# Second cross-attention of a fused two-layer kernel: key tiles taken in pairs, self-attention steps placed anew

## The chip, the cores and the metric

One Trainium2 chip, one core. The metric is the device time of one launch in microseconds; lower is better. The kernel before takes 3031.07 us (median of 3 runs, 3030.28 to 3032.9).

## The reference, cut to what matters

x is 32 sequences of 64 rows of 256; ctx is 32 contexts of 1601 keys of 256. Each of six layer parts has a layer norm ahead and a residual around it. Layer 0 is a cross-attention over ctx, a causal self-attention and a quantised FFN; layer 1 is the part at issue, and a mixture-of-experts FFN follows it.

```
# layer 1, cross-attention: 16 heads of 16
kv = mem @ W_kv;  q = x @ W_q
attn = softmax(q k^T * 16**-0.5)          # 64 queries x 1601 keys per head
out  = (attn @ v) @ W_proj + b_proj       # x += out
# layer 1, self-attention: 16 heads of 16, causal, 64 rows
Q, K, V = per-head products of xn with Wq, Wk, Wv
attn = softmax(mask(Q K^T * 16**-0.5));  out = attn @ V
x += (out, transposed and reshaped) @ W_O
```

## The kernel before, in words

Five engine programs (PE, ACT, DVE, POOL, SP) are written out by hand, each in its own order; they meet only at semaphores, and an engine that waits holds all that stands behind it. x is held in SBUF as 16 tiles of 128 rows, two batches each. Phase B, the subject here, runs `pe_pair`, `act_pair`, `vec_pair` and `pool_pair` once per tile: 16 pairs of batches. The first pair has no tile to finish, the last has none to prepare.

A batch has two stages. In the **maxima stage** PE multiplies the queries by all keys in 16 units (`maxima`, L1133) for DVE to take row maxima, and between the units projects keys and values of the next batch (`project`, pieces K and V, into banks 6 and 5); ACT evacuates them (`evac`), POOL makes the low parts `k_lo` (`split_keys`, L527). It ends with DVE writing `shift`. In the **score stage** (PE L1278 to L1295) 13 key tiles `t` of 128 keys follow. "Scores" of a tile are 2 bf16 matmuls that lay down the shift (L1283) and 12 fp32r matmuls (L1287), all on 64 rows of the array, in two row groups side by side; they fill banks 0, 1 or 2, 3 (`t % 2`). ACT takes the exponential of the tile, 128x1024, into `probs` (L825). "Weigh" of a tile is 16 fp32 matmuls of 64 columns on 32 columns of the array (L1153, each recorded as two), four column groups side by side, into bank 4. PE's order is scores(t), weigh(t-1), then `finish(g)` and `prepare(g)` with `g = 13 * batch + t`.

`finish` spreads over both batches what is left for the tile before: at g=0 the output projection of the cross-attention (L1173); DVE adds it and the bias to x and takes the layer norm; g=2 the transposition of xn (L957), g=3 Q, K, V (L1183, L1185), and then four quarters q of four heads: S4(q), the scores of the self-attention (L1195, one fp32 matmul 128x128 by 512 columns, at g=4, 6, 8, 10), which needs `skbd`, the keys spread by head by POOL (`spread_keys`, L553). On DVE masking (L1672), maximum (L1675), and its negative (L1677); on ACT four exponentials with sums accumulated (L790); on PE the transposition P4T(q) (L1203, g=6, 8, 10, 12); on ACT its copy (L794); on PE the product with V, O4(q) (L1214, g=7, 9, 11, 13); on DVE a copy (L1686); on PE the transposition O4T(q) (L1218, L1222), on DVE the division into `cat` (L1691), and at g=16 the product with W_O (L1232).

`prepare` makes the queries of the next tile: layer norm at g=17, 18, transposition at g=19, PE's product at g=20 (L1244), that is at t=7 of the second batch. ACT copies it (L802, L804), POOL makes `q_lo` (`split_queries`) and then `qbd_hi` and `qbd_lo` (`spread_queries`, L540), on which the next pair's first maxima wait (L1252, L1253). In between ACT rounds the next context to `ctx_hi` in four parts (`round_ctx`, L767, after tiles 1, 2, 6, 7) and POOL makes `ctx_lo` (`split_ctx`, L533); SP loads `ctx_raw` again when two parts are done. POOL's order at the end of a pair is split_ctx(2), split_ctx(3), split_queries, spread_queries(0).

Of the kernel before, what the change touches and what calls it, by code (L numbers as in the profile page):

```python
# [71 lines left out]
CTX_STEPS = (1, 2, 6, 7)  # L72
PROBS = 3
# [42 lines left out]
def build(nc, io, out):  # L116
    ctx = ExitStack()
    with ctx:
# [28 lines left out]
        attn_ch = sb("attn_ch", [P, KT, P])  # L147
# [3 lines left out]
        bias_p = sb("bias_p", [P, D])  # L151
# [62 lines left out]
        inv_sb = sb_b("inv", [P, D])  # L214
        attn4 = sb_b("attn4", [P, 4, P])
# [5 lines left out]
        hq_buf = sb("hq_buf", [P, 2048])  # L221
        identb = sb("identb", [P, P], BF16)
# [53 lines left out]
        skbd = [sideB[:, 1792 + 512 * n:2304 + 512 * n].rearrange("p (h t) -> p h t", h=HPQ) for n in range(2)]  # L276
        v4 = sideB[:, 2816:3088]
        p4T = sideB[:, 3072:3584].rearrange("p (h t) -> p h t", h=HPQ)
        k_raw = [sideB[:, 768 + 512 * n:1280 + 512 * n] for n in range(2)]
        wkv_raw = probs[:, 0, :]  # L280

        def vals_of(n, t):
            all_of = vals[:, n, 0:KEY_TILES * HEADS * VW].rearrange("p (t h d) -> p t h d", h=HEADS, d=VW)
            return all_of[:, t, :, :]

# [7 lines left out]
        def unit_parts(m):  # L293
# [9 lines left out]
            qkv_ps qkv_ready ss_ps snmax_ready sp_ready spT_ps spT_ready so_ps  # L303
# [4 lines left out]
            po_ps sqkv_ps sqkv_ready skbd_ready s4_ps s4_masked p4_ready p4T_ps p4T_ready o4_ps weighed4_ready o4T_ps cat_ready wo_ps  # L308
# [19 lines left out]
            (wo[:, :, :], io["w_o"]), (bias_p[:, :], io["b_p"]), (convw[:, :, :], io["conv_w"]), (convb[:, :], io["conv_b"])]  # L328
# [9 lines left out]
        def _(sp):  # L338
# [20 lines left out]
            for h in range(HEADS):  # L359
                g, j = divmod(h, 4)  # L360
                sp.dma_start(w_cp4[32 * j:32 * j + HD, g, :], io["w_cp"][h % HPT * HD:h % HPT * HD + HD, h // HPT, :]).then_inc(s.cp_in, 16)

# [55 lines left out]
        def _(g):  # L418
# [29 lines left out]
            g.wait_ge(s.consts_ready, NCONST)  # L448
            g.memset(w_cp4[:, :, :], 0.0).then_inc(s.cp_zero, 1)
# [73 lines left out]
            bt = (qb, sqk, s4p, scp, ctp, kp)  # L523
# [29 lines left out]
            def spread_keys(q):  # L553

                a, h = divmod(q * HPQ, HPT)
                if q >= 2:
                    g.wait_ge(s.s4_ps, s4p.up())
                g.tensor_tensor(skbd[q % 2], skT[:, a, None, :].broadcast_to([P, HPQ, P]),  # L558
                                head_of[:, h:h + HPQ, None].broadcast_to([P, HPQ, P]), ALU.mult).then_inc(s.skbd_ready, 1)

            def pool_pair(first, last):
# [19 lines left out]
                if not last:  # L581
# [3 lines left out]
                    rsqrt()  # L585
                    split_ctx(2)
# [65 lines left out]
        def _(act):  # L652
# [124 lines left out]
            def finish(g):  # L777

                if g == 2:
                    copy_xnT(7)  # L780
                if g == 3:
# [4 lines left out]
                if g in (5, 7, 9, 11):  # L786
                    n = (g - 5) // 2 % 2
                    act.wait_ge(s.s4_masked, T["s4"].up())
                    for k in range(HPQ):
                        act.activation(s4[n][:, k, :], s4[n][:, k, :], ACT.Exp, bias=s4_nmax[n][:, k:k + 1], scale=HD ** -0.5,  # L790
                                       accum_out=s4_sum[n][:, k:k + 1]).then_inc(s.p4_ready, 1)
                if g in (6, 8, 10, 12):
                    act.wait_ge(s.p4T_ps, T["p4T"].up())
                    act.copy(p4T.rearrange("p h t -> p (h t)"), bank(7)).then_inc(s.p4T_ready, 1)  # L794

            def prepare(g):

                if g == 19:
                    copy_xnT(7)
                if g == 20:  # L800
                    act.wait_ge(s.qB_ps, T["qB"].up())
                    act.mul(qT.rearrange("p k t -> p (k t)"), bank(7, 256), HD ** -0.5).then_inc(s.qB_ready, 1)  # L802
                    act.wait_ge(s.qB_ready, T["qmul"].up())
                    act.copy(q_hi[:, :, :].rearrange("p k t -> p (k t)"), qT.rearrange("p k t -> p (k t)")).then_inc(s.q_hi_ready, 1)  # L804
# [5 lines left out]
            def act_pair(first, last):  # L810
                for b in range(2):
# [9 lines left out]
                    for t in range(KEY_TILES):  # L821
                        g = b * KEY_TILES + t
                        rows = slice(0, keys_of(t))
                        act.wait_ge(s.sc_ps, T["sc"].up())
                        act.activation(probs[rows, t % PROBS, :], PS[rows, 1024 * (t % 2):1024 * (t % 2) + 1024],  # L825
                                       ACT.Exp).then_inc(s.pr_ready, 1)
                        if not first:
                            finish(g)
                        if not last:
                            if g == 20:  # L830
                                act.wait_ge(s.qbd_lo_ready, T["qbd"].up())
                                T["qbd"].up()
# [8 lines left out]
            prepare(19)  # L841
            prepare(20)
# [15 lines left out]
            for g in range(17):  # L858
                finish(g)
# [62 lines left out]
        def _(pe):  # L922
# [5 lines left out]
                         attn=dict(B=2), sums=dict(B=2), sqkv=dict(B=3), skbd=dict(B=QUARTERS), s4_masked=dict(B=QUARTERS), p4=dict(B=QUARTERS * HPQ), p4T=dict(B=QUARTERS),  # L928
# [230 lines left out]
            def end_batch(n, fin):  # L1159

                pe.wait_ge(s.sums_ready, T["sums"].up())
                if n == 0 and fin:
                    pe.wait_ge(s.p4T_ready, T["p4T"].now() + 1)
                pe.matmul(bank(7, D), spread[:, :, :].rearrange("p j d -> p (j d)"), sums_sb[:, :], start=True, stop=True).then_inc(s.den_ps, 1)

            def finish(g):

                if g == 0:

                    pe.wait_ge(s.attn_ready, T["attn"].up(2))  # L1170
                    pe.wait_ge(s.cp_in, 16 * HEADS)
# [3 lines left out]
                if g == 2:  # L1175
                    transpose_xn(7)
                if g == 3:
# [9 lines left out]
                if g in (4, 6, 8, 10):  # L1187
                    q = (g - 4) // 2
                    if q == 0:
                        pe.wait_ge(s.k_lo_ready, T["k_sb"].now())  # L1190
# [14 lines left out]
                if g in (7, 9, 11, 13):  # L1205
                    q = (g - 7) // 2
                    if q:
                        pe.wait_ge(s.weighed4_ready, T["weighed4"].up())
                    if q in (0, 3):
                        pe.wait_ge(s.v_ready, T["v_sb"].now())  # L1210
                    pe.wait_ge(s.p4T_ready, T["p4T"].up())
                    for k in range(HPQ):
                        mine = (q * HPQ + k) * HD
# [3 lines left out]
                    if q:  # L1217
# [747 lines left out]
```

## Time and profile before

| | |
|---|---|
| median of 3 runs | 3031.07 us |
| the profiled execution's own time | 3030.97 us |
| its span, first to last instruction | 3029.2 us |
| PE, PEld busy | 2598.6 us (86%), 2161.2 us (71%) |
| DVE, ACT, POOL busy | 1550.3 (51%), 1403.8 (46%), 930.9 us (31%) |

Busy times of PE are modelled from records of pipelined matmuls, so in this document PE's order is read by starts: from the start of one group to the start of the next. A row "x32" merges 32 instructions. "[0.61 <-POOL ...]" is idle time ahead of the row and what ended it.

### The profile page before, as it was taken

What the parts mean: (1) busy time and instruction counts of PE and PEld (TensorE: products, weight loads), DVE (VectorE), ACT (ScalarE), POOL (GpSimd) and SP (SyncE); (2) the same over time, 40 slices, a digit from 0 to 9 for tenths busy, and PEclk for the clock granted to TensorE, in tenths of its full rate; (3) what the DMA queues carried; (4) which work ended last, traced back from release to release, by engine and by line L of the source; (5) the groups of instructions that cost most, each with busy time, mean ns of one, the idle gap of its engine ahead of it and who ended that gap; (6) DMA issues with size and microseconds to landing.
All of it is one profiled execution on the core that took longest, in us unless ns stands there. A gap on an engine that the chain in (4) does not pass through costs nothing.

```text
span 3029.2 us, 75593 instructions
## 1 busy us (share of the span) xinstructions
PE 2598.6 (86%) x32048; PEld 2161.2 (71%) x32052; DVE 1550.3 (51%) x2693; ACT 1403.8 (46%) x2563; POOL 930.9 (31%) x867
## 2 busy tenths in 40 slices
PE   6999832248999999999999999999999973699997
PEld 3555411137888888888888888888888743699997
DVE  3443377724445355455454454454454534477775
ACT  1222211125555555655655656656556431456564
POOL 1000034243443442442443443443433202211121
PEclk9999955569999999999999999999999965799999
DMA  8888500031110110100100101101101002466665
GB/s 346 316 317 314 224 0 0 0 112 42 35 35 23 35 34 23 37 32 23 45 24 25 44 23 34 35 23 35 34 23 35 2 1 96 155 215 203 213 198 154
DMA packets 48581, 270.19 MB, mean 89 GB/s; under 512 B 4896, under 2 KB 23584, under 8 KB 33696
## 3 DMA queue, kind: packets, MB, share of 16 engines
q1 hardware_dynamic: 40160, 255.82, 23.4%
q0 software_dynamic: 8160, 10.29, 2.2%
q8 instruction: 237, 3.88, 0.5%
q14 instruction: 24, 0.20, 0.0%
HBM read 247.58 MB, written 20.61 MB: 89 GB/s over the span
## 4 chain that ended last, share of the span: by engine, by line
issue 38%; PE 27%; POOL 21%; DVE 6%; DMA 3%; ACT 3%; POOLq 1%; SPq 0%; DVEq 0%; ACTq 0%
POOL k_lo L530 7%; POOL ctx_lo L538 6%; PE PS L1025 3%; PE PS L1005 3%; PE PS L1365 2%; PE PS L1366 2%; PE PS L1367 2%; POOL sideB L558 2%; POOL qbd_lo L543 2%; DMA unit_raw<-in_experts 1%; PE PS L1287 1%; PE PS L1382 1%; POOL slots_d L633 1%; PE PS L1384 1%; PE PS L1383 1%
## 5 line engine op out<-in xcount | busy, mean ns | idle before, releaser
L1634 DVE TENSOR_REDUCE mpart<-PS 128x1 f32<-128x802 f32 (+1 forms) x512 | 487.8, 988 | 443.2 <-PE PS L1141 443.0
L825 ACT ACTIVATE probs<-PS 128x1024 f32<-128x1024 f32 (+1 forms) x416 | 425.1, 1022 | 241.9 <-PE PS L1287 236.9
L530 POOL TENSOR_TENSOR k_lo<-sideB,k_hi 128x400 fp32r<-128x400 f32 (+1 forms) x256 | 255.2, 997 | 353.7 <-ACT k_hi L761 353.3
L538 POOL TENSOR_TENSOR ctx_lo<-ctx_raw,ctx_hi 128x801 fp32r<-128x801 f32 x128 | 224.6, 1764 | 430.2 <-ACT ctx_hi L773 430.2
L1287 PE MATMUL PS<-qbd_hi,k_hi 64*128 64x256 f32 (+1 forms) x1664 | 312.1, 372 | 0.0
L1141 PE MATMUL PS<-k_hi,qbd_hi 128*128 128x512 f32 (+2 forms) x1024 | 263.0, 359 | 22.8 <-POOL ctx_lo L538 13.7
L1153 PE MATMUL PS<-probs,vals 128*32 128x64 f32 x13312 | 272.9, 222 | 3.0 <-ACT probs L825 2.2
L760 ACT COPY sideB<-PS 128x400 f32<-128x400 f32 (+1 forms) x256 | 126.6, 494 | 275.4 <-PE PS L1121 275.4
L1153 PEld LDWEIGHTS PS<-probs,vals 128*32 128x32 f32 x13312 | 205.3, 109 | 66.5 <-ACT probs L825 14.0
L1128 PE MATMUL PS<-wkv_hi,ctx_hi 128*128 128x256 f32 (+1 forms) x832 | 236.4, 284 | 0.0
L1130 PE MATMUL PS<-wkv_hi,ctx_lo 128*128 128x256 f32 (+1 forms) x832 | 234.3, 282 | 0.0
L1287 PE MATMUL PS<-qbd_hi,k_lo 64*128 64x256 f32 (+1 forms) x1664 | 233.9, 278 | 0.0
L1287 PE MATMUL PS<-qbd_lo,k_hi 64*128 64x256 f32 (+1 forms) x1664 | 233.6, 277 | 0.0
L1129 PE MATMUL PS<-wkv_lo,ctx_hi 128*128 128x256 f32 (+1 forms) x832 | 233.2, 280 | 0.0
L763 ACT COPY vals<-PS 128x512 f32<-128x512 f32 x192 | 113.0, 589 | 214.2 <-PE PS L1130 214.2
L1141 PEld LDWEIGHTS PS<-k_hi,qbd_hi 128*128 128x128 f32 x1024 | 177.6, 192 | 47.4 <-DVE mpart L1634 24.7
L1365 PE MATMUL PS<-xT_hi,unit_hi 128*128 128x256 f32 x736 | 209.1, 284 | 2.2 <-DVE xT_lo L1848 2.2
L1366 PE MATMUL PS<-xT_lo,unit_hi 128*128 128x256 f32 x736 | 209.3, 284 | 0.0
L1367 PE MATMUL PS<-xT_hi,unit_lo 128*128 128x256 f32 x736 | 208.8, 284 | 0.0
L1119 PE MATMUL PS<-ctx_hi,wkv_hi 128*128 128x400 f32 (+1 forms) x512 | 186.9, 365 | 18.6 <-POOL ctx_lo L538 18.6
L644 POOL DMA_INDIRECT sum_d<-scaled,xg x46 | 75.8, 1647 | 347.7 <-DVE scaled L1885 340.7
L1121 PE MATMUL PS<-ctx_hi,wkv_lo 128*128 128x400 f32 (+1 forms) x512 | 178.4, 348 | 0.0
(324 smaller groups left out, 6174.3 us busy)
## 6 DMA issues: line engine op xcount, KB each, us to landing
unit_raw<-in_experts SPq DMA_DIRECT2D x46, 1536.0 KB, 7.1
ctxN<-in_ctxN SPq DMA_DIRECT2D x16, 3328.0 KB, 10.8
ctxT<-in_ctxT SPq DMA_DIRECT2D x16, 3204.0 KB, 10.4
ctx_raw<-in_ctxT SPq DMA_DIRECT2D x64, 801.0 KB, 4.5
slots_d<-pad_rows SPq DMA_DIRECT2D x2, 2990.0 KB, 18.5
xg<-slots_d SPq DMA_DIRECT2D x23, 260.0 KB, 2.8
x<-in_x SPq DMA_DIRECT2D x1, 2048.0 KB, 9.6
sum_d<-x SPq DMA_DIRECT2D x1, 2048.0 KB, 6.3
```

What stands on the lines that cost most here:

```text
L530: g.tensor_tensor(k_lo[:, n, a, c:c + width], k_raw[p % 2][:, 0:width], k_hi[:, n, a, c:c + width].bitcast(F32), ALU.subtract).then_inc(s. ...
L538: g.tensor_tensor(ctx_lo[:, a, cols], ctx_raw[:, cols], ctx_hi[:, a, cols].bitcast(F32), ALU.subtract).then_inc(s.ctx_lo_ready, 1)
L825: act.activation(probs[rows, t % PROBS, :], PS[rows, 1024 * (t % 2):1024 * (t % 2) + 1024], ACT.Exp).then_inc(s.pr_ready, 1)
L1128: pe.matmul(to, ctx_hi[:, k, keys], wkv_hi[:, k, D:2 * D], start=k == 0, stop=False)
L1130: mm = pe.matmul(to, ctx_lo[:, k, keys], wkv_hi[:, k, D:2 * D], start=False, stop=k == KT - 1)
L1141: mm = pe.matmul(at, qbd_hi[:, n, pair // 4, (pair % 4) * P:(pair % 4) * P + P], k_hi[:, n, pair // 4, c:c + width], start=True, stop=True)
L1153: mm = pe.matmul(bank(4, S, slice(32 * j, 32 * j + 32), g * S), vals[rows, n, mine:mine + 32], probs[rows, t % PROBS, at_head(h):at_head(h ...
L1287: mm = pe.matmul(bank(2 * (t % 2) + r, 256, rows, a * 256), keys_part[part, n, a, keys], queries[part, n, a, r * 256:r * 256 + 256], start ...
L1365: pe.matmul(to, hi[:, k, cols], tokens_hi[:, k, :], start=k == 0, stop=False)
L1366: pe.matmul(to, hi[:, k, cols], tokens_lo[:, k, :], start=False, stop=False)
L1367: mm = pe.matmul(to, lo[:, k, cols], tokens_hi[:, k, :], start=False, stop=k == KT - 1)
L1634: v.tensor_reduce(mpart[:, pair, half:half + 1], PS[:, at:at + width], AX, ALU.max).then_inc(s.mx_red, 1)
```

## The change

On PE the score stage takes the key tiles two by two: scores(t), scores(t+1), `beside(t)`, weigh(t-2), weigh(t-1), `beside(t+1)`, where `beside` calls `finish` and `prepare` with a place of 14 to a batch. `probs` gets a fourth buffer. S4 becomes two matmuls of 64 rows by 256 columns, side by side in banks 5 and 6, and `skbd` is half as wide. P4T(3) and what follows move into the second batch, and the queries' product from after 8 tiles' scores and 7 tiles' weighing to after 10 and 6. On ACT both exponentials of a pair stand ahead of the steps; the exponentials of a quarter are one instruction, for which DVE now subtracts the maximum and sums (`centre`, `sums4`). `round_ctx` runs after tile pairs 0 (two parts), 6 and 8. The projection's bias comes in as a row of its weights, which takes one DVE addition away. `k_raw` lies in `probs[1]`. POOL waits for the layer norm before it goes on.

```diff
-CTX_STEPS = (1, 2, 6, 7)
-PROBS = 3
+CTX_AT = {0: (0, 1), 6: (2,), 8: (3,)}
+PROBS = 4
+PLACES = KEY_TILES + 1
+S4_AT = (6, 8, 10, 12)
+P4T_AT = (8, 10, 12, PLACES + 2)
+O4_AT = (9, 11, 13, PLACES + 3)
+O4T_AT = (11, 13, PLACES + 3, PLACES + 5)
+WO_AT = PLACES + 6
+QUERY_AT = (PLACES + 7, PLACES + 8)
...
             def pool_pair(first, last):
...
                     rsqrt()
+                    g.wait_ge(s.xn_ready, xnp.up())
...
+            def exp_p4(q):      # ACT
+                act.wait_ge(s.s4_centred, T["s4"].up())
+                act.activation(s4[q % 2], s4[q % 2], ACT.Exp, scale=HD ** -0.5).then_inc(s.p4_ready, 1)
...
+                if window in (8, 10, 12, PLACES + 2):
+                    copy_p4T()
+                if window in (6, 8, 10, PLACES):
+                    exp_p4((6, 8, 10, PLACES).index(window))
...
+                    for t in range(0, KEY_TILES, 2):      # ACT
+                        for one in range(t, min(t + 2, KEY_TILES)):
+                            rows = slice(0, keys_of(one))
+                            if one == 1:
+                                act.wait_ge(s.k_lo_ready, T["k_lo"].now())
+                            act.wait_ge(s.sc_ps, T["sc"].up())
+                            act.activation(probs[rows, one % PROBS, :], PS[...], ACT.Exp).then_inc(s.pr_ready, 1)
                         if not first:
-                            finish(g)
+                            finish(b * PLACES + t)
                         if not last:
-                            prepare(g)
-                            if t in CTX_STEPS:
-                                round_ctx(CTX_STEPS.index(t))
+                            prepare(b * PLACES + t)
+                            for part in CTX_AT.get(t, ()):
+                                round_ctx(part)
...
+                if place in S4_AT:      # PE
+                    q = S4_AT.index(place)
...
+                    elif q == 1:
+                        pe.wait_ge(s.s4_masked, T["s4_masked"].up())
                     else:
-                        pe.wait_ge(s.s4_masked, T["s4_masked"].up())
+                        pe.wait_ge(s.weighed4_ready, T["weighed4"].up())
                     pe.wait_ge(s.skbd_ready, T["skbd"].up())
-                    pe.matmul(bank(6), sqT[:, q // 2, :], skbd[q % 2].rearrange("p h t -> p (h t)"), start=True, stop=True)
+                    for r in range(2):
+                        part = slice(64 * r, 64 * r + 64)
+                        mm = pe.matmul(bank(5 + r, 2 * P), sqT[part, q // 2, :], skbd[q % 2][part, :, :]..., skip_group_check=True)
...
                 pe.wait_ge(s.shift_ready, T["shift"].up(4))
-                for t in range(KEY_TILES):
+                def scores(t):
...
+                    if t >= 2:
+                        pe.wait_ge(s.pr_ready, exps_before + t - 1)
...
-                    if t >= 1:
-                        weigh(n, t - 1)
-                    if not first:
-                        finish(n * KEY_TILES + t)
-                    if not last:
-                        prepare(n * KEY_TILES + t)
+                for t in range(0, KEY_TILES, 2):
+                    for one in range(t, min(t + 2, KEY_TILES)):
+                        scores(one)
+                    beside(n * PLACES + t)
+                    if t:
+                        weigh(n, t - 2)
+                        weigh(n, t - 1)
+                    beside(n * PLACES + t + 1)
...
+            def centre(q):      # DVE
+                v.wait_ge(s.s4_masked, T["masked"].up())
+                v.tensor_reduce(s4_max, s4[q % 2], AX, ALU.max).then_inc(s.vec_step, 1)
+                v.wait_ge(s.vec_step, own())
+                v.tensor_tensor(s4[q % 2], s4[q % 2], s4_max[:, :, None].broadcast_to([P, HPQ, P]), ALU.subtract).then_inc(s.s4_centred, 1)
+            def sums4(q):
+                v.wait_ge(s.p4_ready, T["p4"].up())
...
+                v.tensor_reduce(s4_sum[q % 2], s4[q % 2], AX, ALU.add).then_inc(s.vec_step, 1)
+                v.wait_ge(s.vec_step, own())
+                v.reciprocal(s4_inv[q % 2], s4_sum[q % 2]).then_inc(s.vec_step, 1)
...
+                if window == 8:
+                    mask_keys(1)
+                    centre(1)
+                    sums4(0)
+                    take(0)
+                if window == 10:
+                    mask_keys(2)
+                    centre(2)
+                    sums4(1)
+                    take(1)
+                    divide(0)
+                if window == 12:
+                    mask_keys(3)
+                    sums4(2)
+                    take(2)
+                    divide(1)
+                if window == PLACES:
+                    centre(3)
```

## Rows read from the trace of the kernel before

**Rows 1.** Busy time by stretch, a pair's two score stages: window, length, engines, clock, DMA.
```profile
1261.18:1293.35 32.17, 31.46 (x638) 23.85 (x639) 10.04 (x27) 24.33 (x57) 11.93 (x10) 1.00 0.17 54
...
1320.51:1345.68 25.17, 25.12 (x605) 20.56 (x605) 2.82 (x10) 16.79 (x21) 12.40 (x10) 1.00 0.21 68
```
**Rows 2.** PE in order of time, first batch: start, us, engine, line, operation, count.
```profile
1264.14 0.39 PE L1283 MATMUL PS<-shift,onesb 64*128 64x512 bf16 x2
...
1273.27 1.10 PE L1195 MATMUL PS<-sideB 128*128 128x512 f32 x2 [0.61 <-POOL sideB L558]
...
1275.90 0.39 PE L1283 MATMUL PS<-shift,onesb 64*128 64x512 bf16 x2
...
1276.60 0.28 PE L1287 MATMUL PS<-qbd_lo,k_hi 64*128 64x256 f32 x2
1276.71 0.28 PE L1287 MATMUL PS<-qbd_hi,k_lo 64*128 64x256 f32 x2
1276.92 0.65 PE L1153 MATMUL PS<-probs,vals 128*32 128x64 f32 x32
1277.51 1.12 PE L1195 MATMUL PS<-sideB 128*128 128x512 f32 x2
1278.47 0.60 PE L1203 MATMUL PS<-ident,sideB 128*128 128x128 f32 x4
1279.00 0.39 PE L1283 MATMUL PS<-shift,onesb 64*128 64x512 bf16 x2
...
1290.15 0.65 PE L1153 MATMUL PS<-probs,vals 128*32 128x64 f32 x32
...
1290.62 0.40 PE L1214 MATMUL PS<-sideB 128*32 128x128 f32 x8
...
1291.21 0.41 PE L1283 MATMUL PS<-shift,onesb 64*65 64x512 bf16 x2
```
**Rows 3.** PE in order of time, end of the second batch.
```profile
1336.35 1.16 PE L1244 MATMUL PS<-xnT,w_cq 128*128 128x128 f32 x8
...
1344.97 0.65 PE L1153 MATMUL PS<-probs,vals 128*32 128x64 f32 x32
1345.68 0.61 PE L1141 MATMUL PS<-k_hi,qbd_hi 128*128 128x512 f32 x2
```
**Rows 4.** ACT in order of time, both batches.
```profile
1265.28 1.02 ACT L825 ACTIVATE probs<-PS 128x1024 f32<-128x1024 f32 x1 [1.93 <-PE PS L1287]
...
1279.11 0.59 ACT L794 COPY sideB<-PS 128x512 f32<-128x512 f32 x1 [0.22 <-PE PS L1203]
1279.59 0.86 ACT L773 CAST ctx_hi<-ctx_raw 128x801 fp32r<-128x801 f32 x1
1280.35 1.03 ACT L825 ACTIVATE probs<-PS 128x1024 f32<-128x1024 f32 x1
1281.27 0.40 ACT L790 ACTIVATE sideB<-sideB,small 128x128 f32<-128x128 f32 x1
...
1337.55 0.38 ACT L802 ACTIVATE sideB<-PS 128x256 f32<-128x256 f32 x1 [0.64 <-PE PS L1244]
```
**Rows 5.** DVE in order of time, first batch.
```profile
1274.40 0.69 DVE L1672 TENSOR_TENSOR sideB<-PS,causal 128x512 f32<-128x512 f32 x1 [7.00 <-PE PS L1195]
1275.13 0.69 DVE L1675 TENSOR_REDUCE small<-sideB 128x4 f32<-128x512 f32 x1
1275.85 0.17 DVE L1677 TENSOR_SCALAR small<-small 128x4 f32<-128x4 f32 x1
...
1280.96 0.29 DVE L1686 COPY xnT<-PS 128x128 f32<-128x128 f32 x1 [0.56 <-PE PS L1214]
```
**Rows 6.** POOL in order of time, end of the second batch, and the next first batch.
```profile
1339.21 1.61 POOL L538 TENSOR_TENSOR ctx_lo<-ctx_raw,ctx_hi 128x801 fp32r<-128x801 f32 x1 [1.55 <-ACT ctx_hi L773]
...
1343.52 1.90 POOL L543 TENSOR_TENSOR qbd_lo<-q_lo,head_of 128x1024 fp32r<-128x1024 f32 x1
...
1378.79 3.91 POOL L538 TENSOR_TENSOR ctx_lo<-ctx_raw,ctx_hi 128x801 fp32r<-128x801 f32 x2 [0.18 <-ACT ctx_hi L773]
```

More of the change, by code:

```diff
@@ L275, in build @@
         s4 = [sideB[:, 768 + 512 * n:1280 + 512 * n].rearrange("p (h t) -> p h t", h=HPQ) for n in range(2)]
-        skbd = [sideB[:, 1792 + 512 * n:2304 + 512 * n].rearrange("p (h t) -> p h t", h=HPQ) for n in range(2)]
+        skbd = [sideB[:, 2304 + 256 * n:2560 + 256 * n].rearrange("p (h t) -> p h t", h=2) for n in range(2)]
         v4 = sideB[:, 2816:3088]
+        attn4 = sideB[:, 1792:2304].rearrange("p (g t) -> p g t", g=4)
         p4T = sideB[:, 3072:3584].rearrange("p (h t) -> p h t", h=HPQ)
-        k_raw = [sideB[:, 768 + 512 * n:1280 + 512 * n] for n in range(2)]
+        k_raw = [probs[:, 1, 512 * n:512 * n + 512] for n in range(2)]
         wkv_raw = probs[:, 0, :]
@@ L857, in _ @@
             copy_sums()
-            for g in range(17):
-                finish(g)
+            for window in range(0, PLACES + 4, 2):
+                finish(window)
             for c in range(CHUNKS):
@@ L1250, in pe_batch @@
                 count[0] = 0
+                if n == 0:
+                    pe.wait_ge(s.x_done, T["x_done"].now())
                 pe.wait_ge(s.k_lo_ready, T["k_sb"].now())
@@ L1277, in pe_batch @@
                 pe.wait_ge(s.shift_ready, T["shift"].up(4))
-                for t in range(KEY_TILES):
+                exps_before = T["pr"].now()
+                def scores(t):
                     rows = slice(0, keys_of(t))
@@ L1289, in pe_batch, with beside @@
                     mm.then_inc(s.sc_ps, 1)
-                    if t >= 1:
+                def beside(place):
+                    if not first:
+                        finish(place)
+                    if not last:
+                        prepare(place)
+                for t in range(0, KEY_TILES, 2):
[4 more added lines that the diff above has]
+                        weigh(n, t - 2)
                         weigh(n, t - 1)
-                    if not first:
-                        finish(n * KEY_TILES + t)
-                    if not last:
-                        prepare(n * KEY_TILES + t)
+                    beside(n * PLACES + t + 1)
             def pe_pair(first, last):
@@ L1301, in _ @@
             pe.wait_ge(s.x_done, XDONE_F)
-            prepare(19)
-            prepare(20)
+            for place in QUERY_AT:
+                prepare(place)
             count[0] = 0
@@ L1315, in _ @@
             weigh(1, KEY_TILES - 1)
-            end_batch(1, True)
-            for g in range(17):
-                finish(g)
+            end_batch(1)
+            for place in range(WO_AT + 1):
+                finish(place)
             for c in range(CHUNKS):
@@ L1713, in vec_pair @@
                     maxima(b, before is None)
-                    for t in range(KEY_TILES):
+                    for t in range(0, KEY_TILES, 2):
                         if before is not None:
-                            finish(b * KEY_TILES + t, before)
+                            finish(b * PLACES + t, before)
                         if after is not None:
-                            prepare(b * KEY_TILES + t, after)
-            prepare(17, x[:, 0, :])
-            prepare(18, x[:, 0, :])
+                            prepare(b * PLACES + t, after)
+            prepare(PLACES + 4, x[:, 0, :])
             v.wait_ge(s.wkv_hi_ready, 1)
@@ L1731, in _ @@
             end_batch(1)
-            for g in range(17):
-                finish(g, x[:, TILES - 1, :])
+            for window in range(0, PLACES + 8, 2):
+                finish(window, x[:, TILES - 1, :])
             v.wait_ge(s.x_done, XDONE_B)
```

229 lines of the change are left out of this document (111 added, 118 removed).

## The prediction

> **What bounds the kernel now.** I read the page's busy table first, then the stretches of one pair, then each engine in order of time over that pair. Of a pair's two score stages the first lasts 32.17 us and the second 25.17, and PE is busy in all but 0.71 and 0.05 of them, at a granted clock of 1.00, which is 2.4 GHz; ACT works 24.33 and 16.79 of them, DVE and POOL less [rows 1]. So PE's own order sets the pace there, and ACT is next. The two maxima stages are the rest of the pair's 111.66 us; the change moves nothing on PE in them.
>
> PE's cost is read from start to start. Scores to weigh is 1.02 us; weigh to a full-array group 0.59; S4 to P4T 0.96; P4T to scores 0.53 [rows 2]. Where the shape of the array's tiles changes there is a loss: within scores the pairs start 0.11 apart, but the first weighing matmul comes 0.21 after the last pair, and weigh followed by O4, in the same 128*32 shape, takes 0.47 in place of 0.59 [rows 2]. So a change of shape costs about 0.10 behind scores and 0.12 behind weigh. Weigh shows also that fp32 matmuls on different column groups run side by side: 32 of them begin and make way in 0.47.
>
> Two other things hold the stage. PE waits 0.61 for `skbd` ahead of S4(0) [rows 2]. And at the end of the second batch POOL is just in time: `qbd_lo` ends at 1345.42, and PE's next batch starts at 1345.68, 0.71 behind a weigh group that elsewhere takes 0.59 [rows 3, 6]. That chain (query matmuls, ACT's copies and ctx_hi(3), ctx_lo(3), q_lo, qbd_hi, qbd_lo) runs from 1336.35 to 1345.68, 9.33 us, and has no slack.
>
> **Gains on PE, first batch of a middle pair.** Six joins of scores with scores, 0.10 each, and six of weigh with weigh, 0.12 each: 1.32. Scores to scores isn't in the trace; I take 0.92, between 0.90 (the sum of its streams) and 1.02. Four S4 stand right behind scores in the same 64-row shape: 0.40. S4 itself: before, two passes of 512 columns; after, on each of two row groups two passes of 256. If the groups overlap as weigh's do, it takes half the streaming, 0.96 to 0.53; if the second waits for the first group's last pass 0.74, if nothing overlaps 0.96. I take 0.53, by weigh: 1.72 in all, with 0 as the other end. The wait for `skbd` goes (0.61): it is half as wide and S4(0) comes after tile 7. P4T(3) leaves for the second batch: 0.53. Together 4.58 us.
>
> The bias addition and its share of the layer norm's chain lie beside scores 2, 3 and weigh 0, 1: nothing on PE, and the chain gets shorter. POOL's new wait for xn holds ctx_lo(0) and (1) back by half a microsecond; behind them stand `spread_keys` and the next load of `ctx_raw`, both wanted only at tile pair 6, so I price it at nothing; if that cover were gone, ACT's ctx_hi(2) would be late, and O4(0) with it, by as much. The fourth buffer of `probs`, `k_raw` in `probs[1]` and the one DMA more are worth nothing: ACT's wait for `k_lo` ahead of tile 1 ends in the maxima stage.
>
> **New waits, first batch.** ACT's order decides. Count from the start of S4(0). DVE's mask starts 1.13 behind S4 now [rows 2, 5]; half the streaming makes it 0.70. Reduce 1.43, subtract 2.15 (new, taken as the mask's 0.69, bounds 0.3 and 1.4), done 2.84. ACT: exponential of the quarter at 2.90 (128x512, taken 0.60 like the copy of that size, bounds 0.40 and 1.02), ctx_hi(2) 3.40, exponential of tile 8 4.16, tile 9 5.08, copy of P4T(0) 6.00 to 6.59, from steps of 0.76 and 0.92 [rows 4]. PE needs it after S4 0.53, two weighs 1.06, two scores 1.84, S4 0.53, P4T 0.53, two weighs 0.94: 5.43. O4(0) starts at 6.70, a wait of 1.27. Behind it on PE stand scores 10 and everything else. For quarter 1 the same chain is just in time. S4(3) waits for `take(1)`: DVE from S4(2) on: mask 0.70, reduce, subtract, sum (0.72 each) to 3.59, reciprocal, copy 0.29 to 4.10 [rows 5]; PE is there at 0.53 + 0.53 + 0.94 + 0.59 (O4, O4T [rows 2]) + 0.92 = 3.51: wait 0.64. First batch: -4.58 + 1.27 + 0.64 = -2.67.
>
> **Second batch.** Joins -1.32; P4T(3) +0.53; O4(3) now behind weigh in the same shape -0.12; the old wait of 0.12 at the end is part of (c) below, -0.12. Then three waits. (a) Scores 2 needs the exponential of tile 0, which starts 1.14 behind its scores and takes 1.02 [rows 2, 4]: 2.20 instead of 1.84, +0.35. In the first batch the projection L1173 covers this. (b) ACT does tiles 0 and 1 at 1.14 and 2.07, then the exponential of quarter 3 at 2.99, ctx_hi(0) 3.49, ctx_hi(1) 4.25, tiles 2 and 3 at 5.01 and 5.93, and only then the copy of P4T(3), 6.85 to 7.44. PE, with scores 2 and 3, P4T(3) and two weighs, is at O4(3) at 5.62 and waits to 7.55: +1.93. (c) The queries' product stands later on PE. From its start PE has 1.1 + 3 scores (0.92, 1.02, 1.02) + 6 weighs (0.47, 0.59, 0.47, 0.59, 0.47, 0.71) = 7.35 to the next batch, while the chain behind it is what it was, 9.33; ACT's tile 9 is out of its way. PE waits +1.98 there, with the whole next maxima stage behind it. Sum: -1.32 - 0.12 - 0.12 + 0.53 + 0.35 + 1.93 + 1.98 = +3.23 us.
>
> **Sum.** A middle pair: -2.67 + 3.23 = +0.56, times 14 = +7.8. First pair (nothing to finish): joins -2.64, scores 2 and 4 wait 0.75 in each batch, query chain +1.98: +0.8. Last pair: no ctx_hi ahead of tile 8, so first batch -3.4, second -0.2. The last tile's steps after the loop run by themselves: a shorter S4, spread and exponential against a subtraction and a sum in DVE's line; I take 0, bounds -4 and +4. The sum is 7.8 + 0.8 - 3.6 = +5.0. The profiled execution took 3030.97 us (span 3029.2), the median is 3031.07, so the same sum serves both: 3036.
>
> **A collision that is possible.** Two ctx_lo take 3.91, 1.95 each, in the stretch where DVE normalizes, and one alone takes 1.61 [rows 6]: DVE and POOL slow each other somewhere. A subtraction with both operands in SBUF is new on DVE. What it would cost is rival D. The Trainium skill ("SBUF - State Buffer", section "Who interferes with whom") says that a DVE instruction with two SBUF inputs and a GpSimd instruction that reads SBUF exclude one another for the whole instruction, whichever starts first. The masking addition has one input in PSUM, so by that rule the change brings in a collision that the kernel before doesn't have.
>
> **Rivals.**
> A, the forecast, 3036 (its own range 3024 to 3049), chance 0.40.
> B, faster: ACT doesn't hold PE. If O4(0) and O4(3) find their copies ready, 15 x 1.27 + 14 x 1.93 = 46 us go: 2990; with half of it 3013. For it: ACT is idle 8 us of each score stage [rows 1]. Against: its order is fixed, and the copy stands behind two exponentials of 0.92. It decides whether the copy of P4T(3) ends before weigh 1 does. Chance 0.22.
> C, faster: the queries' chain gets shorter than 9.33, or the wait is absorbed: 15 x 1.98 = 30 us, 3007. Against: POOL's five steps are untouched. Chance 0.08.
> D, slower: DVE's subtraction meets ctx_lo or `spread_keys` on POOL. centre(2) runs some 0.9 us after spread_keys(3) ends by my count, centre(1) inside ctx_lo(2). Each hit costs up to 1.61 [rows 6], and what reaches PE is that at O4(0) and S4(3): one hit a pair in full 15 x 1.61 = 24, 3060. It decides from a POOL instruction that begins before the subtraction does. Chance 0.20.
> E, slower, the change doesn't do what it says: the two halves of S4 don't overlap and scores behind scores still cost 1.02: (4 x 0.43 + 16 x 0.10) a pair, of which the waits hide about a third: +33, 3069; with S4 in 0.74 alone +9, 3046. Chance 0.10.
>
> **How the numbers follow.** This kernel's runs can tell 0.2%, 6 us: 3025 to 3037.1 is no change. Of A 0.02 is below, 0.20 in it, 0.18 above. B and C are faster but for 0.03 that end in the middle. D and E are slower but for 0.02. Faster 0.29, same 0.25, slower 0.46. The time is A's, 3036. Range: below, B's half and C are to be held and B's full size left out, 2999; above, D in full, 3060.
>
> **What would show it.** Start to start: scores to scores 0.92, weigh to weigh 0.47, S4 to the next group 0.53. Idle ahead of O4(0) and O4(3) put down to ACT's copy (1.3, 1.9), ahead of S4(3) to DVE's copy (0.6), ahead of the first maxima of a pair to `qbd_lo` (2.0). First score stage 29.5 us, second 28.4, pair 112.2. DVE's subtraction at 0.69. The forecast is wrong if the pair is under 111 or over 113.5, or if these waits stand elsewhere.

## The result, and the profile after

The changed kernel takes 3044.34 us (median of 6 runs, 3040.91 to 3046.99) against 3032.11 us of the kernel before on the same chip: a ratio of 1.0040, 95% interval 1.0027 to 1.0053. It is slower by 12 us. The forecast was 3036 in 2999 to 3060, and "slower" had the largest chance.

In the profiled execution (3046.99 us, span 3044.9, before 3029.2) PE is busy for less time, and the time is longer. First the busy table's row, then four stages by stretch with the columns of [rows 1]: both score stages of a pair, the maxima stage behind them, and the second score stage of the next pair.

```profile
PE 2553.1 (84%) x32176; PEld 2164.1 (71%) x32180; DVE 1614.8 (53%) x2741; ACT 1338.9 (44%) x2115; POOL 901.2 (30%) x868
```
```profile
1156.29:1185.20 28.91, 28.03 (x642) 22.99 (x643) 11.29 (x25) 20.55 (x28) 10.07 (x10) 1.00 0.19 59
1212.35:1240.74 28.39, 24.43 (x608) 20.71 (x609) 4.81 (x13) 17.87 (x23) 12.40 (x10) 1.00 0.19 60
1240.74:1268.86 28.12, 27.65 (x195) 25.41 (x196) 21.11 (x29) 11.19 (x24) 11.26 (x10) 0.94 0.01 2
1326.24:1356.14 29.90, 25.94 (x608) 22.03 (x609) 4.81 (x13) 17.95 (x23) 12.41 (x10) 0.94 0.18 58
```

Two things are to be seen. The first stage went from 32.17 to 28.91 us and the second from 25.17 to 28.39 [rows 1], so a pair in which nothing else happens (the sum of its four stages' medians) is 111.65 us, as before (111.66). And some stages are longer by themselves: the maxima stage of 27.17 is 28.12 here, the second score stage of 28.39 is 29.90, and in both the granted clock is 0.94 in place of 1.00. The trace's clock shows why: in the 16 pairs it stands at 0.5 (1.2 GHz) for 14 stretches, 13 of 3.4 us and one of 6.8; the kernel before has none (both are low over the first 4.6 us of the pairs and once at their very end, which is left out of all counts here).

PE's steps in the first batch (start, length, count, idle ahead). They answer to [rows 2]:

```profile
1168.05 0.39 PE L1319 MATMUL PS<-shift,onesb 64*128 64x512 bf16 x2
...
1169.00 0.39 PE L1319 MATMUL PS<-shift,onesb 64*128 64x512 bf16 x2
...
1169.94 0.59 PE L1224 MATMUL PS<-sideB 64*128 64x256 f32 x4
1170.46 1.10 PE L1181 MATMUL PS<-probs,vals 128*32 128x64 f32 x64
1171.49 0.39 PE L1319 MATMUL PS<-shift,onesb 64*128 64x512 bf16 x2
```

Scores to scores is 0.94 to 0.95, S4 to the next group 0.52, two weighs 1.03, and no wait stands ahead of S4(0). A later pair shows the wait at O4(0) in its usual size:

```profile
1282.51 0.60 PE L1224 MATMUL PS<-sideB 64*128 64x256 f32 x4
...
1287.05 1.10 PE L1181 MATMUL PS<-probs,vals 128*32 128x64 f32 x64
1289.17 0.42 PE L1245 MATMUL PS<-sideB 128*32 128x128 f32 x8 [1.02 <-ACT sideB L804]
```

In the second batch PE waits at O4(3), and then at the next pair's first maxima, where [rows 3] had no wait:

```profile
1217.14 1.10 PE L1181 MATMUL PS<-probs,vals 128*32 128x64 f32 x64
1219.94 0.43 PE L1245 MATMUL PS<-sideB 128*32 128x128 f32 x8 [1.71 <-ACT sideB L804]
...
1237.57 1.10 PE L1181 MATMUL PS<-probs,vals 128*32 128x64 f32 x64
1240.74 0.61 PE L1169 MATMUL PS<-k_hi,qbd_hi 128*128 128x512 f32 x2 [2.07 <-POOL qbd_lo L561]
```

What holds them is the order on ACT, with rows that answer to [rows 4]. Two roundings of the context (L794) stand ahead of the exponentials of tiles 2 and 3, and these ahead of the copy (L804). Later ACT sits 2.62 us in front of the copy of xn, with the third rounding behind it, which needed no xn:

```profile
1215.88 1.61 ACT L794 CAST ctx_hi<-ctx_raw 128x801 fp32r<-128x801 f32 x2
1217.39 1.94 ACT L856 ACTIVATE probs<-PS 128x1024 f32<-128x1024 f32 x2
1219.21 0.60 ACT L804 COPY sideB<-PS 128x512 f32<-128x512 f32 x1
...
1229.55 0.37 ACT L692 COPY xnT<-PS 128x256 f32<-128x256 f32 x1 [2.62 <-PE PS L985]
1229.82 0.86 ACT L794 CAST ctx_hi<-ctx_raw 128x801 fp32r<-128x801 f32 x1
...
1233.02 0.41 ACT L833 CAST q_hi<-sideB 128x256 fp32r<-128x256 f32 x1
1233.33 0.86 ACT L794 CAST ctx_hi<-ctx_raw 128x801 fp32r<-128x801 f32 x1
```

So the fourth subtraction on POOL stands between `q_hi` and the queries' own steps, as in [rows 6]:

```profile
1234.27 1.61 POOL L556 TENSOR_TENSOR ctx_lo<-ctx_raw,ctx_hi 128x801 fp32r<-128x801 f32 x1 [1.91 <-ACT ctx_hi L794]
1235.83 0.73 POOL L567 TENSOR_TENSOR q_lo<-sideB,q_hi 128x256 f32<-128x256 f32 x1
1236.72 1.91 POOL L561 TENSOR_TENSOR qbd_hi<-q_hi,head_of 128x1024 fp32r<-128x1024 f32 x1 [0.16 <-POOL q_lo L567]
1238.59 1.90 POOL L561 TENSOR_TENSOR qbd_lo<-q_lo,head_of 128x1024 fp32r<-128x1024 f32 x1
```

PE's waits over the pairs, with their sum, number and longest:

```profile
PE PS L1245 <- ACT sideB L804: 36.7, 29, 1.7
PE PS L1169 <- POOL qbd_lo L561: 31.9, 15, 2.8
```

### The profile page after: what moved, and what is told of

It is laid out like the page before. It is cut to its first block, busy times and chain, and to the rows that moved or that the text cites. A ratio compares the mean times of both kernels' runs of the same rounds, so it can differ in the third digit from the quotient of the medians.

```text
span 3044.9 us, 75411 instructions
## 1 busy us (share of the span) xinstructions
PE 2553.1 (84%) x32176; PEld 2164.1 (71%) x32180; DVE 1614.8 (53%) x2741; ACT 1338.9 (44%) x2115; POOL 901.2 (30%) x868
## 4 chain that ended last, share of the span: by engine, by line
issue 41%; PE 28%; POOL 18%; DVE 6%; ACT 3%; DMA 3%; POOLq 1%; SPq 0%; DVEq 0%; ACTq 0%
POOL k_lo L548 7%; POOL ctx_lo L556 5%; PE PS L1053 3%; PE PS L1033 3%; PE PS L1410 2%; PE PS L1411 2%; PE PS L1412 2%; POOL qbd_lo L561 2%; PE PS L1169 1%; PE PS L1323 1%; PE PS L1427 1%; PE PS L1428 1%; PE PS L1429 1%; DMA unit_raw<-in_experts 1%; POOL sideB L575 1%
## 5 line engine op out<-in xcount | busy, mean ns | idle before, releaser
L856 ACT ACTIVATE probs<-PS 128x1024 f32<-128x1024 f32 (+1 forms) x416 | 409.5, 1025 | 186.8 <-PE PS L1323 186.8
L548 POOL TENSOR_TENSOR k_lo<-probs,k_hi 128x400 fp32r<-128x400 f32 (+1 forms) x256 | 253.7, 991 | 338.5 <-ACT k_hi L782 338.3
L1169 PE MATMUL PS<-k_hi,qbd_hi 128*128 128x512 f32 (+2 forms) x1024 | 269.9, 366 | 53.5 <-POOL qbd_lo L561 31.9
L781 ACT COPY probs<-PS 128x400 f32<-128x400 f32 (+1 forms) x256 | 126.6, 494 | 347.1 <-PE PS L1149 346.1
L1181 PE MATMUL PS<-probs,vals 128*32 128x64 f32 x13312 | 234.3, 221 | 2.6 <-issue 2.5
L1181 PEld LDWEIGHTS PS<-probs,vals 128*32 128x32 f32 x13312 | 197.4, 110 | 46.6 <-issue 30.1
L1319 PE MATMUL PS<-shift,onesb 64*128 64x512 bf16 (+1 forms) x832 | 165.0, 393 | 18.4 <-DVE shift L1695 13.5
L1148 PE MATMUL PS<-ctx_lo,wkv_hi 128*128 128x400 f32 (+1 forms) x512 | 180.4, 352 | 0.0
```

The source lines that it names most:

```text
L548: g.tensor_tensor(k_lo[:, n, a, c:c + width], k_raw[p % 2][:, 0:width], k_hi[:, n, a, c:c + width].bitcast(F32), ALU.subtract).then_inc(s. ...
L856: act.activation(probs[rows, one % PROBS, :], PS[rows, 1024 * (one % 2):1024 * (one % 2) + 1024], ACT.Exp).then_inc(s.pr_ready, 1)
L1169: mm = pe.matmul(at, qbd_hi[:, n, pair // 4, (pair % 4) * P:(pair % 4) * P + P], k_hi[:, n, pair // 4, c:c + width], start=True, stop=True)
L1181: mm = pe.matmul(bank(4, S, slice(32 * j, 32 * j + 32), g * S), vals[rows, n, mine:mine + 32], probs[rows, t % PROBS, at_head(h):at_head(h ...
```

## The experiments

Theory: the new order gives PE 4 to 5 us a pair; three waits of ordered queues (O4(0), O4(3), first maxima) take all of it back; and the two long ones make the granted clock fall, which is the loss. Rivals are with each. Stage lengths below are medians of the stages without low clock, unless said. Numbers compared are medians of different runs; on each chip the kernel before ran beside and took 3031.57 to 3033.41 us.

### The copy ahead of the context's rounding

```diff
-CTX_AT = {0: (0, 1), 6: (2,), 8: (3,)}
+CTX_AT = ({0: (0, 1), 6: (2,), 8: (3,)}, {2: (0, 1), 6: (2,), 8: (3,)})   # by batch
```

> One edit of the changed kernel: in the second batch ScalarE rounds the first two parts of the context in window 2, behind its copy of quarter 3's transposed weights, and not in window 0 ahead of the exponentials of tiles 2 and 3. My theory (the wait of the fourth weighted sum is 1.5 us of rounding in front of the copy): that idle of 1.71 us falls under 0.3, the second score stage goes from 28.4 to 26.7 us, and the granted clock no longer falls in that stage; 15 pairs x 1.7 + 5 stretches x 1.5 = 33 us: 3012 us. Rival (waits of an ordered queue return at the next place, here the queries' chain at the first maxima): the stage is shorter but that wait grows by as much, 3035 to 3044 us.

Measured: 3025.71 us, ratio to the kernel before 0.9972 (0.9960 to 0.9985). The wait at O4(3) went: what is left over for O4 on ACT is 15.8 us in place of 36.7. The second stage fell by 1.5 us to 26.9. The wait at the maxima stayed (33.2 us over the pairs, 31.9 in the changed kernel), and the gain of the clock did not come: 11 stretches in place of 14, three of them of 6.8 us, cost 18 us as the 14 did. The second row is a maxima stage with one of these, 2.4 us longer than 27.17:

```profile
1207.04:1233.90 26.86, 24.41 (x608) 20.71 (x609) 4.81 (x13) 17.86 (x23) 12.43 (x10) 1.00 0.20 64
1345.57:1375.17 29.60, 29.13 (x196) 26.62 (x197) 21.07 (x29) 11.19 (x24) 11.22 (x10) 0.89 0.00 1
```

The wait did not return elsewhere, so the rival is out. The forecast of 3012 was 14 too low: 7.5 of that is the clock, 4 is that the stage fell by 1.5 us in 14 pairs where I had reckoned 1.7 in 15, and the rest is less than these runs scatter (3017 to 3034). The wait before the maxima alone is enough to make the clock fall.

### The context's last parts ahead of the copy of xn

In the second batch ACT's window 6 rounds parts 2 and 3 first:

```diff
-CTX_AT = {0: (0, 1), 6: (2,), 8: (3,)}
+CTX_AT = ({0: (0, 1), 6: (2,), 8: (3,)}, {0: (0, 1), 6: (2, 3)})
...
+                        ahead_of_rest = t == 6 and b in (1,)
+                        if not last and ahead_of_rest:
+                            for part in CTX_AT[b].get(t, ()):
+                                round_ctx(part)
                         if not first:
                             finish(b * PLACES + t)
                         if not last:
                             prepare(b * PLACES + t)
```

> One edit of the changed kernel: in the second batch ScalarE rounds the last two parts of the context in window 6 ahead of the copy of the normalized tile, so GpSimd's subtractions for them are done before the queries come. My theory (the first maxima wait for 1.6 us of subtraction that stands ahead of the queries' in GpSimd's queue, behind a rounding that waited 2.6 us for the transposition): the idle of 2.07 us before the first maxima falls under 0.3, 15 x 2.0 = 30 us, and 8 stretches of lower clock (0.95 each) go: 38 us, 3007 us. Rival (the transfer of the context's second half lands later than window 6, so the same wait only moves): 3030 to 3044 us.

Measured: 3004.21 us, ratio 0.9897 (0.9881 to 0.9914). No wait on `qbd_lo` is left in the pairs and the second stage is 26.25, 2.1 less, so the rival is out. Six stretches of low clock remain, and each begins 0.8 to 1.4 us after the end of a wait of 1.71 us at O4(3), which is still there. The first row is such a stage (27.86, clock 0.94), the second the maxima stage behind it, undisturbed:

```profile
1202.22:1230.08 27.86, 25.97 (x609) 22.03 (x609) 4.82 (x13) 17.95 (x23) 12.68 (x10) 0.94 0.20 62
1230.08:1257.28 27.20, 26.21 (x201) 24.30 (x196) 21.06 (x29) 11.29 (x25) 11.22 (x10) 1.00 0.00 1
```

### All three waits away

Both edits, and in the first batch part 2 ahead of quarter 0's exponentials in window 6.

> Both edits above, and in the first batch the third part of the context is rounded ahead of quarter 0's exponentials, so that the exponentials of tiles 8 and 9 and the copy for the first weighted sum come 0.8 us sooner. My theory: all three waits go together, 15 x (1.7 + 2.05 + 0.8) = 68 us, and 12 us of lower clock: 3044 - 80 = 2964 us, pair 107.1 us. Rival (they share one cover, removing one exposes another): between 3000 and 3012 us.

Measured: 2971.39 us, ratio 0.9796 (0.9779 to 0.9812). It beats both kernels, and lies 62 us under the kernel before on the same chip (3033.41). No stretch of low clock in the pairs. The stages are 28.17 and 24.73, the pair 107.25, 4.4 under the changed kernel's: 0.8 in the first stage, and 3.7 in the second, which is the 1.5 and the 2.1 of the two edits alone. So the waits were independent and each was worth about its size. O4(0) comes 5.89 us after S4(0) in place of 6.66 (1267.57 - 1261.68, 1289.17 - 1282.51):

```profile
1248.02:1276.19 28.17, 27.82 (x642) 22.76 (x643) 11.27 (x25) 20.49 (x28) 10.40 (x10) 1.00 0.19 61
1303.35:1328.07 24.72, 24.34 (x609) 20.69 (x609) 4.81 (x13) 17.62 (x23) 12.59 (x10) 1.00 0.21 70
```
```profile
1261.68 0.59 PE L1229 MATMUL PS<-sideB 64*128 64x256 f32 x4
...
1267.57 0.42 PE L1250 MATMUL PS<-sideB 128*32 128x128 f32 x8 [0.25 <-ACT sideB L804]
```

### The waits stay, PE is kept busy in them

```diff
+            def fill(times):
+                for _ in range(times):
+                    pe.matmul(bank(5, P, at=P), ident[:, :], ones[:, :], start=True, stop=True)
...
                         pe.wait_ge(s.v_ready, T["v_sb"].now())      # O4(3)
+                        fill(6)
                     pe.wait_ge(s.p4T_ready, T["p4T"].up())
...
                 pe.wait_ge(s.k_lo_ready, T["k_sb"].now())           # first maxima
+                if n == 0 and not first:
+                    pe.wait_ge(s.v_ready, T["v_sb"].now())
+                    fill(7)
                 pe.wait_ge(s.qbd_hi_ready, T["qbd"].up())
```

> The changed kernel with TensorE kept busy in its two long waits: 6 matmuls of 128x128 float32 on constants, into an unread part of a bank, ahead of the fourth weighted sum's wait for its copy, and 7 ahead of the first maxima's wait for the queries. No wait is removed and no other work changed. My theory (the lower clock comes from these two idle times): the stretches at 0.5 in the cross-attention go from 14 to 3 or fewer, the stages stay 28.4 and 28.9 us, 3044 - 12 = 3032 us. Rival 1 (the clock falls for some other reason, such as the mean load of a pair): 14 stretches or more and 3044 us. Rival 2 (the fill delays what waits behind it): up to 3060 us.

Measured: 3022.20 us, ratio 0.9962 (0.9948 to 0.9976): 22 us less than the changed kernel, by adding work. No stretch of low clock in the pairs. The steps still wait for the same copies: O4(3) starts 2.72 us after the weighs (2.80 in the changed kernel).

```profile
1208.77 1.10 PE L1181 MATMUL PS<-probs,vals 128*32 128x64 f32 x64
1209.80 1.60 PE L1194 MATMUL PS<-ones,ident 128*128 128x128 f32 x12
1211.49 0.43 PE L1250 MATMUL PS<-sideB 128*32 128x128 f32 x8
```
```profile
1203.99:1232.14 28.15, 27.72 (x634) 23.73 (x635) 4.81 (x13) 17.87 (x23) 12.27 (x10) 1.00 0.19 61
1232.14:1259.31 27.17, 26.17 (x195) 24.26 (x196) 21.06 (x29) 11.20 (x24) 11.61 (x10) 1.00 0.00 1
```

This shows that the clock fell because PE stood idle there (in the changed kernel 13 of the 14 stretches began between 0.2 us ahead of and 2.1 us behind the end of one of these two waits, and one behind another idle of 1.27 us), and prices it: the stages of 14 pairs had 19.3 us over their undisturbed lengths in the changed kernel and 2.4 here. Of the 19.3, 15.7 lie in the 13 stages with low clock; the last stretch, of 6.8 us, stands in the last pair and cost 2.4 more, so the clock is worth 18 us. Another 0.24 a pair comes from the second stage (28.39 to 28.15): behind the ends of the ACT and POOL instructions that release it PE starts 0.05 and 0.10 us later here, 0.14 and 0.26 in the changed kernel. My 12 us was too low because I had taken it from the medians' difference.

### Key tiles no longer in pairs

On the kernel without the waits:

```diff
                 for t in range(0, KEY_TILES, 2):
-                    for one in range(t, min(t + 2, KEY_TILES)):
-                        scores(one)
+                    scores(t)
+                    if t:
+                        weigh(n, t - 2)
+                    if t + 1 < KEY_TILES:
+                        scores(t + 1)
                     beside(n * PLACES + t)
                     if t:
-                        weigh(n, t - 2)
                         weigh(n, t - 1)
```

> The kernel without the three waits (e3_all_waits, 2971.4 us), with TensorE's order of the key tiles undone: score tile, weighted tile, score tile, weighted tile, and not two and two. Everything else, the places of the self-attention too, stays. My theory (each join of score and weighted matmuls costs 0.11 us of TensorE, 12 more of them in each score stage): the stages grow by 1.3 us each, 30 stages: 2971 + 40 = 3011 us. Rival (a join costs nothing by itself and the gain of the first stage was the four halved instructions and moved work): 2971 to 2980 us.

Measured: 3042.51 us, ratio 1.0035 (1.0021 to 1.0049). The second stage grew by 1.50 us. I had counted 12 more joins; the edit makes 10, since scores 0 and 1 and weighs 10 and 11 stay together. From start to start two scores and two weighs take 3.00 us in pairs and 3.23 in turn, so a join costs 0.12 and ten 1.2; the other 0.3 is at O4(3), which waits 0.52 here. First without, then with this edit:

```profile
1322.99 0.39 PE L1324 MATMUL PS<-shift,onesb 64*128 64x512 bf16 x2
...
1325.99 0.41 PE L1324 MATMUL PS<-shift,onesb 64*65 64x512 bf16 x2
```
```profile
1346.83 0.39 PE L1324 MATMUL PS<-shift,onesb 64*128 64x512 bf16 x2
...
1350.06 0.41 PE L1324 MATMUL PS<-shift,onesb 64*65 64x512 bf16 x2
```

The first stage grew by 3.53, and that I had not forecast:

```profile
1267.08:1298.78 31.70, 29.51 (x642) 23.21 (x643) 12.80 (x25) 20.74 (x28) 10.07 (x10) 1.00 0.17 54
...
1325.93:1352.15 26.22, 25.52 (x608) 20.91 (x609) 4.81 (x13) 18.21 (x23) 12.42 (x10) 1.00 0.21 66
```

DVE is busy 12.80 us there and not 11.27. Its subtraction of the maxima (L1719) started 0.04 us behind POOL's subtraction of the context and took 2.10 us:

```profile
1059.43 2.10 DVE L1719 TENSOR_TENSOR sideB<-sideB,small 128x512 f32<-128x512 f32 x1
```
```profile
1059.39 1.60 POOL L556 TENSOR_TENSOR ctx_lo<-ctx_raw,ctx_hi 128x801 fp32r<-128x801 f32 x1 [0.75 <-ACT ctx_hi L794]
```

That is rival D's collision. In all 14 meetings of this execution the subtraction ended 0.55 us after POOL's instruction: it did next to nothing until that was through. The Trainium skill ("SBUF — State Buffer", section "Who interferes with whom") says just that of a VectorE instruction with two SBUF inputs and a GpSimd instruction that reads SBUF; the traces agree, with 2.10 against 0.69 us.

### The same, with the collision moved away

```diff
-                        ahead_of_rest = t == 6 and b in (0, 1)
+                        ahead_of_rest = t == 6 and b in (1,)
```

> e5_alternate (3042.5 us, first score stage 31.7 us) with one edit: in the first batch ScalarE rounds the third part of the context behind quarter 0's exponentials again, so that GpSimd's subtraction for it no longer starts 0.04 us ahead of VectorE's subtraction of the maxima. Theory (the two instructions exclude one another, rival D of the prediction: VectorE's took 2.10 us in place of 0.69 in e5_alternate): it falls to 0.69, the idle of 0.67 us ahead of the first transposition goes, the copy for the first weighted sum comes 1.4 - 0.84 = 0.6 us sooner, the first score stage falls to 30.4 to 31.0, and the time by 10 to 20 us to 3028 us. Rival (the extra 2.2 us of that stage are ScalarE's order and the moved places alone): the subtraction's length has no effect on TensorE, the stage stays 31.7 or grows by the 0.84 us of rounding ahead of the exponentials, 3042 to 3054 us.

Measured: 3031.77 us, ratio 0.9998 (0.9988 to 1.0007), 10.7 us under the kernel with the collision. The mean of the subtraction over the pairs went from 1045 to 692 ns, the stage from 31.70 to 31.04. So a collision of 1.41 us on DVE reaches PE with 0.66 us net of the rounding moved back. The stage is still 2.87 over the 28.17 of the kernel with pairs: 0.76 of that is between S4(0) and O4(0), where the rounding stands ahead again (6.65 us here, 5.89 there), and up to 1.2 are the ten joins; the rest, about 0.9, I have not separated.

```profile
1265.53:1296.57 31.04, 29.43 (x642) 23.19 (x643) 11.28 (x25) 20.81 (x28) 10.08 (x10) 1.00 0.17 55
```
```profile
L1719 DVE TENSOR_TENSOR sideB<-sideB,small 128x512 f32<-128x512 f32 x56 | 38.7, 692 | 1.9
```

### S4 on all rows

```diff
-                        mm = pe.matmul(bank(5 + r, 2 * P), sqT[part, q // 2, :], skbd[q % 2][part, :, :]...)
+                        mm = pe.matmul(bank(5 + r, 2 * P), sqT[:, q // 2, :], skbd[q % 2][:, :, :]...)
```

> e3_all_waits with the two score matmuls of each self-attention quarter over all 128 rows and not over 64 rows each, so that they can't run beside each other; it sums the scores of the head pairs, so what is computed is changed there, the number and the columns of the instructions are not. My theory (the halves overlap, 0.53 against 0.96 us): each quarter costs 0.43 us more on TensorE, 4 x 0.43 x 15 = 26 us: 2997 us. Rival (the quarter's time lies beside a wait, so it is worth nothing): 2971 us.

Measured: 3004.97 us, ratio 0.9906 (0.9889 to 0.9923), 34 us more than without the edit; what is computed differs, the number and the columns of the matmuls do not. The first stage is 30.75, 2.58 more, where 1.72 was expected. By starts: S4 0.97 against 0.52; the scores ahead of it 0.98 against 0.89, now that S4 has another shape; P4T behind it 0.53 against 0.59; net 0.48 a quarter, 1.9 us, of which some goes into waits that PE had there before: in three of the 15 pairs the subtraction is not hit and the stage is 29.7 to 29.8 us, 1.5 more. The rest, about 1.0, is the collision again: the subtraction took 1.7 to 1.9 us for quarter 0 in most pairs, and O4(0) waited 0.71 in place of 0.25.

```profile
1148.12:1178.85 30.73, 29.80 (x643) 24.62 (x643) 12.34 (x25) 20.71 (x28) 10.08 (x10) 1.00 0.18 56
```

### The exponentials by head again

```diff
-                act.activation(s4[q % 2], s4[q % 2], ACT.Exp, scale=HD ** -0.5).then_inc(s.p4_ready, 1)
+                for k in range(HPQ):
+                    mm = act.activation(s4[q % 2][:, k, :], s4[q % 2][:, k, :], ACT.Exp, bias=s4_nmax[q % 2][:, k:k + 1],
+                                        scale=HD ** -0.5, accum_out=s4_sum[q % 2][:, k:k + 1])
+                mm.then_inc(s.p4_ready, 1)
...
-                v.tensor_tensor(s4[q % 2], s4[q % 2], s4_max[:, :, None].broadcast_to([P, HPQ, P]), ALU.subtract).then_inc(s.s4_centred, 1)
+                v.tensor_scalar(s4_nmax[q % 2], s4_max, -(HD ** -0.5), None, ALU.mult).then_inc(s.s4_centred, 1)
...
-                v.tensor_reduce(s4_sum[q % 2], s4[q % 2], AX, ALU.add).then_inc(s.vec_step, 1)
```

> e3_all_waits with the exponentials of the self-attention as in the kernel before: four instructions of 128x128 with bias and sum each on ScalarE (2.3 us a quarter by the rows of the kernel before, against 0.63 us), and VectorE without the subtraction (0.69 us) and the sum (0.69 us). My theory (ScalarE's queue sets when the weighted sums may start): the copies for quarters 0, 2 and 3 come 1 to 1.5 us later and TensorE waits for them, about 4 us in a pair, and some lower clock: 2971 + 60 = 3030 us, between 2995 and 3045. Rival (ScalarE has room once the context's parts are out of the way, and VectorE's shorter chain gives it back): 2966 to 2976 us.

Measured: 2996.92 us, ratio 0.9881 (0.9864 to 0.9897), 25.5 us more. The stages grew by 0.55 and 1.00 us. ScalarE's queue does set the start of the weighted sums, but I had counted only its 1.7 us more and not that VectorE hands over 0.5 us sooner and that the gaps on ScalarE ahead of quarters 1 and 2 take up the rest. That account is read from one pair and not tested. The one instruction is worth 1.55 us a pair here, less than half of what I said, and the rival's 2966 to 2976 is out too.

```profile
1256.48:1285.12 28.64, 27.81 (x642) 22.83 (x643) 7.96 (x22) 23.41 (x49) 10.08 (x10) 1.00 0.19 60
1312.28:1338.00 25.72, 24.42 (x608) 20.68 (x608) 3.60 (x12) 18.62 (x30) 12.49 (x10) 1.00 0.21 67
```

## Why the prediction was right, and where it was not

The mechanism held: PE's gain in the first stage is paid back at O4(0), O4(3) and the next first maxima, by waits near the sizes forecast. That the kernel came out slower is luck: by these terms alone it would have been some 8 us faster than before, and what made it slower, the granted clock, is in no step of the forecast.

- **Joins, S4, `skbd`, P4T(3): forecast -4.58 us.** Scores to scores 0.94 (0.92), S4 0.52 (0.53), the `skbd` wait gone. Without most of the wait at O4(0) the stage is 28.17, 4.0 under before, with some 0.5 of waits left in it. Undoing the joins costs 0.12 each (0.11), undoing the halves 0.48 a quarter by starts (0.43). Right.
- **O4(0), forecast 6.70 us after S4(0): 6.66.** Right. Its wait was 1.02 and not 1.27, since PE's own steps up to it take 5.64 and not 5.43.
- **S4(3), forecast +0.64 for `take(1)`: about 0.27** (1.20 between the starts of the last scores and S4(3), where it is 0.93 for S4(0)). Too large; this is most of what put the first stage at 29.5 and not 28.9. The sum on DVE started 0.61 behind the subtraction, not 0.72, and the copy 0.10 behind the reciprocal.
- **Second stage, forecast 28.4: 28.39.** O4(3) 2.80 behind the weighs, that is +1.88 (1.93). Scores 2 came 1.29 behind scores 1, +0.35 (0.35). The maxima waited 2.07 (1.98).
- **Middle pair, forecast 112.2: 111.65.** The 0.56 of loss was nothing: 14 pairs are 0 and not +7.8. The first pair gave -0.2 (+0.8). From the last pair's first maxima to the end it is 5.4 us less in the two profiled executions (672.1 and 677.4), although 2.4 us of low clock are in it: -7.7 without (-3.6 forecast, bounds of 4 on its tail). Together -8: with no fall of the clock the forecast's own terms make the change faster. (Ahead of the pairs the changed kernel's profiled execution took 3.8 us more than the one before; the kernels of the experiments, with the same order there, 0.5 to 2.7 more. That is not explained.)
- **Missing: the granted clock.** I priced each wait at its length and took the clock of 1.00 [rows 1] over unchanged. It fell 14 times, 13 of them at the two long waits, and cost 18 us. With some 2 us more in stages without low clock, this turns the -8 into the measured +12. It should have been a rival: PE is idle for 0.71 us at most in the stages of [rows 1], so they could not show what 2 us of idle do.
- **Rival B** was false for this kernel, but is what three moved roundings make of it. **C** was false, POOL's chain took what it did. **D** was true as a mechanism and small: in the changed kernel the subtraction of quarter 1 starts 1.24 us into POOL's instruction in most pairs and takes 0.91 in place of 0.69:

```profile
1288.03 0.91 DVE L1712 TENSOR_TENSOR sideB<-sideB,small 128x512 f32<-128x512 f32 x1
```
```profile
1286.79 1.60 POOL L556 TENSOR_TENSOR ctx_lo<-ctx_raw,ctx_hi 128x801 fp32r<-128x801 f32 x1 [2.97 <-ACT ctx_hi L794]
```

  It reaches nobody: O4(1), which comes from it, has no wait. The experiments that moved things by a microsecond hit it in full. **E** was false in both halves.

What stays open: why the clock falls at one such wait and not at the next, in pairs that are alike (13 times for 29 long waits in the changed kernel), and why the last pair and what follows gained more than forecast.

## What to carry to other kernels

When an order written by hand packs one engine's work more closely, read the other engines' queues for what stands ahead of each hand-over, and move what nobody waits for behind it: three such moves of roundings turned a change of +12 us into -62. Price an idle time of about 2 us on TensorE at more than its length, by what the clock is in the stages behind it. A small instruction on VectorE with both inputs in SBUF is worth placing away from GpSimd's long ones.

## What the hardware showed that was not expected

- After waits of 1.7 to 2.1 us on PE (once 2.8), in a kernel that is otherwise busy, the granted clock went to 0.5 for 3.4 or 6.8 us, in 13 of 29 cases; with those of 1.7 us taken away the other 15 made 11 stretches, with those of 2.1 us taken away the other 14 made 6. Waits of 0.8 to 1.0 us at O4(0), left in the kernel with the filled waits, made none. But shorter ones are not safe: with the key tiles in turn again and the collision, a wait of 0.68 us and one of 1.15 behind it made 2 stretches in 14 pairs, while 14 of 1.24 alone, with the collision moved away, made none. One stretch of 3.4 us costs 0.95 us in a maxima stage of the changed kernel, 1.4 to 1.8 in most of those with the copy ahead, and 1.5 to 1.6 in a second score stage.
- Matmuls on constants in the two waits took 22 us away, 18 of them low clock.
- POOL waits for DVE in the same way: a subtraction of the context that started 0.21 us behind DVE's took 1.94 us in place of 1.61.

```profile
1263.77 0.69 DVE L1717 TENSOR_TENSOR sideB<-sideB,small 128x512 f32<-128x512 f32 x1
```
```profile
1263.98 1.94 POOL L556 TENSOR_TENSOR ctx_lo<-ctx_raw,ctx_hi 128x801 fp32r<-128x801 f32 x1 [1.00 <-ACT ctx_hi L794]
```
